# Scaling and shifting the retention's input on ScalarE instead of VectorE, ahead of the last slot of each step

## What is computed

```python
x = L0_attn_x                      # (4, 1024, 128)
xn = _layernorm(x, axis=-1)
x = x + _L0_attn_ref(xn, ...) + _L0_ffn_ref(xn, ...)
```

```python
residual = x
xn = channel_group_norm(x, norm_g, norm_b, H)      # H = 16 groups of 8 channels
q = l2_normalize(xn @ qw.T)
k = l2_normalize(xn @ kw.T)
v = xn @ vw.T
...                                 # 16 heads, causal, decays gamma**(n-m)
x = residual + (y @ ow.T + ob)
residual = x
xn = channel_group_norm(x, ffn_norm_g, ffn_norm_b, H)
x = residual + (silu(xn @ w1.T + b1) @ w2.T + b2)
```

## Time and profile before

| | us |
|---|---|
| median of three runs | 1102.1 |
| the three runs | 1096.9, 1102.1, 1102.71 |
| span of the profiled execution, first to last instruction | 1096.5 |
| busy in it: PE | 975.7 (89%) |
| DVE | 786.8 (72%) |
| ACT | 684.2 (62%) |
| POOL | 620.7 (57%) |

### The profile page before, as it was taken

One profiled execution on the slowest core, in us unless ns is written; L12 is line 12 of the kernel. 1 busy time (PEld: TensorE's weight loads), 2 busy tenths in 40 slices (PEclk: granted clock), 3 DMA queues, 4 the chain that ended last, 5 costly groups with the idle time before them and its releaser, 6 DMA issues.

```text
span 1096.5 us, 22810 instructions
## 1 busy us (share of the span) xinstructions
PE 975.7 (89%) x8404; PEld 665.2 (61%) x8404; DVE 786.8 (72%) x1257; ACT 684.2 (62%) x1315; POOL 620.7 (57%) x474
## 2 busy tenths in 40 slices
PE   1779889899899899898998996999999999999876
PEld 1447666585686676765855864556565656565552
DVE  5776776766876867767768767696877878797933
ACT  1355745747647567467476575786777777687643
POOL 4575646545655556465456654675756556575600
PEclk9989999999999999999999998999999999999997
DMA  9000000000000000000000000000000000000000
GB/s 286 1 1 1 2 1 1 1 1 0 0 1 0 0 0 0 0 0 0 0 0 0 0 1 1 1 1 1 20 10 10 19 0 19 0 19 0 20 20 10
DMA packets 20403, 12.30 MB, mean 11 GB/s; under 512 B 4578, under 2 KB 19596, under 8 KB 20236
## 3 DMA queue, kind: packets, MB, share of 16 engines
q1 hardware_dynamic: 15108, 10.49, 3.1%
q10 hardware_dynamic: 5256, 1.28, 0.6%
HBM read 9.67 MB, written 2.10 MB: 11 GB/s over the span
## 4 chain that ended last, share of the span: by engine, by line
PE 59%; DVE 19%; ACT 9%; issue 8%; POOL 3%; DMA 1%; DVEq 1%; ACTq 0%; SPq 0%; POOLq 0%
PE pQK L1138 8%; PE pS L1067 4%; DVE m L709 4%; PE pM L1084 4%; PE pS L1041 4%; PE pT L1052 4%; PE pT L1014 3%; PE pM L1208 3%; PE pS L1249 3%; DVE xa L821 3%; PE pV L1104 3%; DVE xa L888 2%; PE pQK L1283 2%; PE pT L1240 2%; PE pS L1028 2%
## 5 line engine op out<-in xcount | busy, mean ns | idle before, releaser
L367 POOL TENSOR_TENSOR rn<-rn,half_neg 128x16 f32<-128x16 f32 x64 | 187.7, 2932 | 5.3
L380 POOL TENSOR_TENSOR m<-m 128x1024 f32<-128x1024 f32 x64 | 151.4, 2365 | 0.0
L365 POOL TENSOR_SCALAR rn<-ss 128x16 f32<-128x16 f32 x64 | 16.8, 263 | 220.9 <-DVE ss L699 219.7
L1138 PE MATMUL pQK<-wqkv,hT 128*128 128x512 f32 x256 | 132.8, 645 | 1.8 <-DVE m L709 1.8
L387 POOL TENSOR_TENSOR qkn<-m,rn 128x1024 f32<-128x1024 f32 x64 | 123.8, 1934 | 6.1 <-POOL m L380 2.0
L719 DVE TENSOR_REDUCE mx<-pS 128x8 f32<-128x1024 f32 x64 | 78.1, 1220 | 67.2 <-PE pS L1041 67.2
L507 ACT ACTIVATE kT<-pT 128x512 f32<-128x512 f32 x64 | 38.2, 597 | 99.1 <-PE pT L1014 98.7
L547 ACT ACTIVATE sq<-pQK 128x1024 f32<-128x1024 f32 x64 | 65.5, 1023 | 43.8 <-PE pQK L1138 43.8
L699 DVE TENSOR_REDUCE ss<-sq 128x16 f32<-128x1024 f32 x64 | 77.5, 1211 | 7.0 <-ACT sq L547 7.0
L419 POOL TENSOR_TENSOR sq<-aqkT,cst 128x512 f32<-128x512 f32 x32 | 33.6, 1051 | 85.9 <-ACT aqkT L611 79.4
L531 ACT ACTIVATE prT<-pT 128x1024 f32<-128x1024 f32 x64 | 65.4, 1022 | 25.2 <-PE pT L1052 24.2
(11 more groups left out here) (172 smaller groups left out, 2409.7 us busy)
## 6 DMA issues: line engine op xcount, KB each, us to landing
x<-in_L_attn_x SPq DMA_DIRECT2D x4, 512.0 KB, 8.2
xs<-in_L_attn_x SPq DMA_DIRECT2D x8, 256.0 KB, 2.7
out<-aqkT SPq DMA_DIRECT2D x8, 256.0 KB, 2.3
wqkv<-in_L_ffn_wqkv SPq DMA_DIRECT2D x2, 768.0 KB, 10.3
tab<-in_k_tab SPq DMA_DIRECT2D x1, 1024.0 KB, 10.2
w<-in_L_ffn_w SPq DMA_DIRECT2D x2, 341.0 KB, 10.7
wo<-in_L_ffn_wo SPq DMA_DIRECT2D x2, 256.0 KB
cst<-in_k_cst ACTq DMA_DIRECT2D x1, 404.5 KB, 4.0
```

The source lines that it names most:

```text
L367: eng.tensor_tensor(rn[:, k % 2, :], rn[:, k % 2, :], half_neg[:, 0:2 * H], ALU.pow).then_inc(S["rn_done"], 1)
L380: eng.tensor_tensor(m1[:, k % 2, :], m1[:, k % 2, :], m2[:, k % 2, :], ALU.add).then_inc(S["add_done"], 1)
L1138: mm = eng.matmul(pQK[:, g * 512:(g + 1) * 512], hT[:, k, :], wqkv[:, l, g * 512:(g + 1) * 512], start=True, stop=True)
```

## The change

The four operations that make xa leave DVE. ACT makes them as four activations of the function Identity, each with a column of gsc[0] as scale and a column of gsh[0] as bias, at the head of its slot 3: behind the exponent of slot 2 and ahead of the evacuation of kT. The wait before them is now for the last use of xa's padded copy in the step before (vx_mm) in place of qkv_mm. In step (0, 0) ACT also waits once for the group norm's columns (gn[0] "done"), which DVE writes in slot 1. Nothing else is moved, and PE still waits for all four xa.

```diff
@@ act_slot, after the shift for k == 0
+            if k == NB - 1 and new and new[0] == 0:
+                if is_start(new):
+                    eng.wait_ge(gn[0]["done"], 1)
+                act_retention_in(eng, new[1])
             turned = at(new, old, k - 2)
...
+        def act_retention_in(eng, t):
+
+            need_apart(eng, A["vx_mm"], 4 * t)
+            for b in range(NB):
+                eng.activation(xa[:, b, :], xnT[:, b, bass.ds(t * P + 1, P)], ACT.Identity, bias=gsh[0][:, b:b + 1],
+                               scale=gsc[0][:, b:b + 1]).then_inc(A["xa"], 1)
...
@@ dve_slot
             retain = k == NB - 1 and new and new[0] == 0
-            if retain:
-                dve_retention_in(eng, new[1])
...
-        def dve_retention_in(eng, t):
-
-            need(eng, A["qkv_mm"], 4 * t)
-            for b in range(NB):
-                eng.tensor_scalar(xa[:, b, :], xnT[:, b, bass.ds(t * P + 1, P)], gsc[0][:, b:b + 1], gsh[0][:, b:b + 1],
-                                  ALU.mult, ALU.add).then_inc(A["xa"], 1)
```

## The result

The changed kernel takes 1067.4 us (median of 4 runs, 1066.5 to 1069.2) where the kernel before takes 1099.5 (4 runs beside it, 1096.9 to 1102.7): a ratio of 0.971, 95% interval 0.968 to 0.973. The profiled spans are 1065.5 and 1096.5 us, 31.0 apart, and the mean granted clock over them is 0.985 in place of 0.972. Lines behind the edit moved by a few: L1014 is L1016 now, L1028 L1030, L1218 L1220, L1231 L1233, L507 and L509 L511 and L513, L831 L833, L719 and L721 L730 and L732.

The account below looks back on a forecast made before the run. PE, busy 89% of the span, was the bound, through its idle time and clock. Seven steps x 4.2 us = 29.4 us off the median 1102.1 gave 1072.7 us, range 1064 to 1085.

Parts of the forecast that it names:

- The four are held up by POOL: DVE's L821 in step (0, 3): the four take 4.86 us beside POOL's add and scale, own work some 1.4.
- d: Delay of kT and qT on ACT behind the four added activations: 0.8 to 1.5 us, taken as 1.3.
- The gain per step: Seven layer-0 steps, at the retention: each 4.2 us shorter, at most 4.55, where POOL's L395 starts at 290.99.
- The formula: Gain reaching the retention per step: 5.5 us less ACT's delay of kT and qT, under POOL's ceiling of 4.55.
- The clock's share: PE's groups L1218 to L1231 behind the idle time: 6.20 us against 4.36 at full clock, 1.84 us per step.
- Step (0, 0) and layer 1: PE doesn't wait for xa in step (0, 0), costed at nothing (1.3 us without cover); layer-1 steps don't change.
- The sum: Whole kernel: 7 x 4.2 = 29.4 us, giving a span of 1067.1 and a time of 1072.7 us.
- The clock falls at the new gap: Rival: PE's 1.3 us idle before L1028 brings the lower clock, 1.84 us back per step, 1085.6 us; chance 0.10.
- A table of its own: Rival: Identity on ACT needs table loads of 1.28 us each, before the four and the next exponent; 1086 us; chance 0.04.
- The stall moves to L719 and L721: Rival: these DVE operations are held beside POOL's add and scale instead, 1.0 us later per step; 1079.7 us; chance 0.04.
- ACT is held: Rival: POOL holds ACT's four until its scaling ends at 290.99, kT 7.7 us later; 1117.5 us, slower; chance 0.05.
- Another wait of PE: Rival: another 4 us wait stands behind xa at L1218, so time stays within 0.5%, 1102 us; chance 0.03.

Follow-up runs that it names:

- the run with six activations: Changed kernel plus two more of the same Identity activations behind ACT's four, into the unread tile hn: 1075.3 us against 1101.9, ratio 0.977.
- the fillers: Kernel before, plus four 128x512 matmuls into pV ahead of L1218 that keep PE busy while it waits for xa: 1088.2 us against 1101.9, ratio 0.988.
- The run with the four in slot 1: Changed kernel with ACT's four activations moved from the head of slot 3 to the head of slot 1: 1071.2 us against 1101.4, ratio 0.974.

## Why the prediction was right

**The mechanism.** "The four are held up by POOL" holds: with the source in PSUM the hold is gone in the same place. Of the four only two are held in each step (2.4 to 2.5 and 2.1 us), and their own work is less than the 1.4 us of the prediction: 1.11 us where nothing holds them. ACT needs longer for the same work (1.64 us), so the gain comes from the hold that is gone and not from a faster engine.

**d.** I took 1.3 us, from 0.8 to 1.5; it was 1.0 (kT at 275.68, 274.68 on this clock). Both columns are there in the row (0.48 us each, the high end), but neighbours overlap by 0.1 each time, and I had granted half of that. "The 0.09 us per column" was right: 0.302 + 2 x 0.09 = 0.48. The Trainium skill (ScalarE: Activation LUTs, section What ACT_TABLE_LOAD costs) gives 186 ns, 0.833 ns per element, some 93 ns for each column operand and some 93 ns of overlap. An estimate from these figures for 128 elements is 479 ns and a start every 386; the rows show 479 and 386.

**The gain per step.** I forecast 4.2 us, with a ceiling of 4.55 by POOL. In step (0, 3) aqk of sequence 1 gained 4.46 and the last L1233 ahead of it 4.57, with L395 0.06 us from the end of L387: the ceiling, since d was small. Over the span it is 31.0 / 7 = 4.4 us, and 4.6 between the steps. The formula held in the run with six activations, which is below the ceiling.

**The clock's share.** The sum had 1.84 us per step, which is the 6.20 us less 4.36 us for the same groups at full clock. The 4.36 were too few: the groups took 4.54 with the fillers and 4.56 with the change, so the clock costs 1.66 us there. The fillers also let the first of them start 0.18 us sooner behind L1014, so that L1235 gains 1.84 in all; that it is the same number is luck. Over the steps the fillers gave 2.0 us each.

**Step (0, 0) and layer 1** were put at nothing, and that is what they cost: the first aqk is 0.3 us later, but PE's turning ahead of it is as well, and layer 1 is the same.

**The sum.** Span 1067.1 forecast, 1065.5 measured. The time, 1072.7 against 1067.4, missed by more, and not by the terms of the change: I set it against a median that lay 5.6 us above the profiled span, and the changed kernel's median is 1.9 above its own. The ratio is the surer quantity: 0.971 x 1102.1 = 1070.1.

**The rivals.** *The clock falls at the new gap:* 1.00 behind 0.85 us and behind 1.61 us. But the witness that I had against it was weak: "PE does nothing for 1.97 us, and the clock stays at 1.00" was one outcome of two at that very place. Had d been 2 us, the conclusion would have rested on luck. *A table of its own:* the count of loads at L483 is 40 as before. *The stall moves to L719 and L721:* 1.23 and 1.22 us beside POOL's two. *ACT is held:* no, but the changed kernel hardly tests it. The prediction let ACT wait for POOL's scaling to end at 290.99, though at 282.88 neither of POOL's large operations runs (L387 ends at 282.36, L380 starts at 286.58). The run with the four in slot 1 tests it, and they keep their length. *Another wait of PE:* the only new one is that for qT.

## What to carry to other kernels

When short operations of one engine have a median far below their maximum, look for another engine's long operation that ends with them. A source in PSUM, another engine or an earlier place each took the hold away or shortened it, and gave nearly the same time here (1067.1, 1067.4 and 1070.1 us). Price a hold by what stands behind it (4.6 us per step in layer 0, 0.2 in layer 1), and price the clock separately, since here it was 2.0 of those 4.6 us. Before claiming a gain find the engine that becomes the bound, which caps it whatever the edit costs.

## What the runs showed of the hardware that I had not expected

- The clock's fall behind an idle time of 2.13 us was not repeatable: 1.00 in one run of the program and 0.62 in the other, and that step was 1.65 us longer.
- A hold isn't found beside every operation of POOL. In step (0, 0) of the kernel before, DVE's four run beside POOL's power of a small tile at their own length (timelines of DVE and POOL):

```profile
69.15 1.11 DVE L821 TENSOR_SCALAR xa<-xnT,gsc,gsh 128x128 f32<-128x128 f32 x4
...
67.34 2.96 POOL L367 TENSOR_TENSOR rn<-rn,half_neg 128x16 f32<-128x16 f32 x1
```

  L367 lasts 2.96 us and the four 1.11.
- The addition and the scaling of 128x1024 aren't the only operations of POOL that go with a longer row of DVE. In the kernel before, the addition of `hidden` and `state`, both in SBUF, takes 691 ns alone and 1.35 us beside POOL's multiplications of 128x512, and the second of these takes 1.49 us in place of 1.04, so here POOL takes longer too (timelines of DVE and POOL):

```profile
303.46 1.35 DVE L852 TENSOR_TENSOR hidden<-hidden,state 128x512 f32<-128x512 f32 x1
...
303.22 1.04 POOL L419 TENSOR_TENSOR sq<-aqkT,cst 128x512 f32<-128x512 f32 x1 [1.69 <-ACT aqkT L611]
304.22 1.49 POOL L423 TENSOR_TENSOR prT<-aqkT,cst 128x512 f32<-128x512 f32 x1
```
- One matmul of 128x512 in f32 took 0.88 us and stands as two rows.
